# xDeepFM forward pass: the eighth broadcast pair moved from TensorE to DMA, with regrouped transfers, accumulator banks, gathers and dumps

## What is computed

```python
emb = tables[feat_idx, sparse]                     # (2048, 26, 32)
x0 = xk = emb
for w, bb in ((conv1_w, conv1_b), (conv2_w, conv2_b)):        # 128 rows each
    hp = einsum('bhd,bmd->bhmd', xk, x0).reshape(-1, h * 26, 32)
    xn = sigmoid(einsum('oi,bid->bod', w, hp) + bb[None, :, None])
    xk, keep = xn[:, :64], xn[:, 64:]              # keep is summed over the 32 and weighted
deep: tanh(x @ W1 + b1) -> tanh(@ W2 + b2) -> tanh(@ W3 + b3) -> @ deep_w   # 845 -> 1024 -> 512 -> 256
```

## Time and profile before

| | us |
|---|---|
| median of 3 runs (1628.97 to 1633.01) | 1631.12 |
| the profiled execution | 1624.22 |
| its span | 1622.4 |
| TensorE busy | 1543.6 (95%) |
| VectorE busy | 1104.7 (68%) |
| GpSimd busy | 709.2 (44%) |
| ScalarE busy | 643.5 (40%) |
| moved by DMA | 319.80 MB, 197 GB/s on average |

### The profile page before, as it was taken

One profiled execution on the slowest core, in us unless ns is written; L12 is line 12 of the kernel. 1 busy time (PEld: TensorE's weight loads), 2 busy tenths in 40 slices (PEclk: granted clock), 3 DMA queues, 4 the chain that ended last, 5 costly groups with the idle time before them and its releaser, 6 DMA issues.

```text
span 1622.4 us, 23599 instructions
## 1 busy us (share of the span) xinstructions
PE 1543.6 (95%) x6584; PEld 656.8 (40%) x6584; DVE 1104.7 (68%) x1017; ACT 643.5 (40%) x904; POOL 709.2 (44%) x600
## 2 busy tenths in 40 slices
PE   0598999999999999999999999999999999999999
PEld 0232333333333333333333333333333336787876
DVE  3276777777777877787777777787877783333332
ACT  2342434344434443434443434434343323344443
POOL 7356565556555556565555646464731110000000
PEclk9899999999999999999999999999999999999999
DMA  6688999999999999999998989898999884634531
GB/s 126 143 183 194 231 214 223 217 231 209 226 212 225 211 224 209 221 214 229 210 228 200 232 201 231 201 240 201 237 203 235 204 210 122 186 120 147 175 104 53
DMA packets 178599, 319.80 MB, mean 197 GB/s; under 512 B 31132, under 2 KB 106812, under 8 KB 178524
## 3 DMA queue, kind: packets, MB, share of 16 engines
q1 hardware_dynamic: 155423, 298.87, 75.0%
q10 hardware_dynamic: 9828, 13.43, 4.1%
q0 software_dynamic: 13312, 7.06, 3.8%
HBM read 297.93 MB, written 21.31 MB: 197 GB/s over the span
## 4 chain that ended last, share of the span: by engine, by line
PE 86%; issue 4%; DVE 3%; another core or an unknown queue 2%; POOL 2%; DMA 1%; SPq 1%; ACT 1%; ACTq 0%; DVEq 0%; POOLq 0%
PE y L751 42%; PE xn L745 19%; PE bc L880 16%; PE bc L731 5%; PE bc L738 3%; DVE hp L692 2%; POOL emb L542 2%; PE bc L723 1%; DVE xb L692 1%; SPq L465 1%; DMA x0t<-x_halves 1%; DMA x_lo<-dense_halves 0%; ACTq L370 0%; DMA emb<-table,idx_stage 0%
## 5 line engine op out<-in xcount | busy, mean ns | idle before, releaser
L692 DVE TENSOR_TENSOR hp<-bc,xk 128x1024 f32<-128x1024 f32 x384 | 453.9, 1219 | 271.3 <-PE bc L731 136.0
L542 POOL DMA_INDIRECT emb<-table,idx_stage x416 | 515.9, 1240 | 145.5 <-issue 126.3
L692 DVE TENSOR_TENSOR xb<-xb,xk 128x1024 f32<-128x1024 f32 x448 | 546.5, 1264 | 27.9 <-ACT xk L927 23.9
L751 PE MATMUL y<-xb,w2s 128*64 128x512 f32 x1792 | 436.0, 601 | 0.0
L745 PE MATMUL xn<-sq,w1s 128*128 128x512 f32 x768 | 369.7, 618 | 4.4 <-issue 4.4
L751 PE MATMUL y<-hp,w2s 128*64 128x512 f32 x1536 | 366.0, 597 | 0.0
L553 POOL TENSOR_TENSOR r<-r 128x512 f32<-128x512 f32 x96 | 123.5, 1287 | 351.0 <-ACT r L932 181.3
L926 ACT ACTIVATE xk<-xn,bias 64x512 f32<-64x512 f32 x128 | 87.4, 683 | 438.5 <-PE xn L745 248.8
L922 ACT ACTIVATE sq<-bc 128x1024 f32<-128x1024 f32 x192 | 182.9, 1026 | 197.5 <-PE bc L738 145.8
L751 PEld LDWEIGHTS y<-xb,w2s 128*64 128x64 f32 x1792 | 116.0, 136 | 248.8 <-issue 201.5
L745 PEld LDWEIGHTS xn<-sq,w1s 128*128 128x128 f32 x768 | 137.5, 192 | 162.6 <-issue 154.8
(11 more groups left out here) (57 smaller groups left out, 843.3 us busy)
## 6 DMA issues: line engine op xcount, KB each, us to landing
xb<-x_rows SPq DMA_DIRECT2D x896, 256.0 KB
w_raw<-W SPq DMA_DIRECT2D x32, 448.0 KB
x0t<-x_halves ACTq DMA_DIRECT2D x252, 52.0 KB
x_halves<-deep_halves SPq DMA_DIRECT2D x30, 384.0 KB
w_raw<-W SPq DMA_DIRECT2D x16, 512.0 KB
emb<-table,idx_stage POOLq DMA_INDIRECT x416
x_hi<-x_halves SPq DMA_DIRECT2D x24, 256.0 KB
x_lo<-x_halves SPq DMA_DIRECT2D x24, 256.0 KB
```

The lines of the kernel that those rows point to most:

```text
L542: nc.gpsimd.indirect_dma_start(out=emb[:, m, :], out_offset=None, in_=table, in_offset=bass.IndirectOffsetOnAxis(ap=idx_stage[:, m:m + 1], ...
L692: nc.vector.tensor_tensor(product(n)[:, :], x[:, :], xk[sl % 2][:, :], ALU.mult).then_inc(multiplied, 1)
L751: last = nc.tensor.matmul(y2[H * c:H * c + H, :], w2s[:, ORDER[n], :], src[:, c * CHUNK:(c + 1) * CHUNK], start=(n == 0), stop=(n == PAIRS ...
```

## The change

- `BY_PE` is now 3, 4, 5, 9, 10 and eight pairs go by DMA, in five groups `COPIED` = (0), (1, 2), (6, 7), (8), (11, 12). `ORDER`, which says which fields a pair number means, is permuted to suit.
- A group is three transfers: one field of each pair into partitions 32 to 95, the other into 0 to 31 and 96 to 127 (`PAIR_ROWS`). SyncE waits once a group, for its last pair, and VectorE waits for a group at its first pair.
- `STEP_WORK` puts both `contract_k` one behind the other, then fills 9, 10, then contracts 0 to 7 in one go; fills are (3, 4, 5) and (9, 10). All three parts of the transposed embedding go into one slot, in one fill.
- `xn` and `y2` become two banks `acc[0]`, `acc[1]` that change places each step: `contract_k(0)` writes the bank that this step's pairs are contracted into afterwards, `contract_k(1)` the other, once the last step's second layer has been read from it. The last step has an order of its own (`FINAL_WORK`), without the squares.
- `deep_step` is step 1 in tile 0 too; `dump_halves` and `dump` stand one behind the other at the end of step 1, after the broadcasts of that step.
- GpSimd's gathers: seven in a row ahead of the step-3 sum instead of three before it and four behind; in tile 0 all 26 for tile 1 are issued in step 0, the last 13 one by one after VectorE's products.
- The first loads of the deep part (`load_x(0)`) are spread over the four steps of the last tile.

```diff
-PAIR_ROWS = ((0, slice(0, H)), (1, slice(H, P)))
+PAIR_ROWS = ((1, slice(QUARTER, 3 * QUARTER)), (0, slice(0, QUARTER)), (0, slice(3 * QUARTER, P)))
-ORDER = [0, 1, 2, 3, 8, 4, 5, 9, 6, 7, 10, 11, 12]
-BY_PE = (3, 4, 6, 7, 9, 10)
+ORDER = [0, 1, 2, 3, 8, 4, 5, 6, 9, 10, 7, 11, 12]
+BY_PE = (3, 4, 5, 9, 10)
+COPIED = ((0,), (1, 2), (6, 7), (8,), (11, 12))
 STEP_WORK = (
     ("fill", (("K", 0), ("K", 1), ("K", 2))),
     ("of_last", (8, 9, 10)),
-    ("fill", (("D", 0), ("D", 1), ("D", 2))),
+    ("fill", (("D", 0),)),
     ("of_last", (11, 12)),
-    ("fill", (3, 4)),
+    ("fill", (3, 4, 5)),
     ("first", 0),
-    ("of_this", (0, 1, 2)),
-    ("fill", (6, 7)),
     ("first", 1),
     ("fill", (9, 10)),
-    ("of_this", (3, 4, 5, 6, 7)),
+    ("of_this", (0, 1, 2, 3, 4, 5, 6, 7)),
 )
-        xn = pb("xn", [P, CHUNK])
-        y2 = pb("y2", [P, CHUNK])
+        acc = [pb(f"acc{i}", [P, CHUNK]) for i in range(2)]
+        terms = acc[(STEPS - 2) % 2]
+        def first_acc(sl, c):
+            return acc[(sl + c) % 2]
             def spread_by_dma(t, sl, i):
+                ns = COPIED[i]
+                at = BY_DMA.index(ns[0])
+                fields = x0_rows[bass.ds(t, 1), :, :].rearrange("t (m e) b -> t m e b", e=ROW)
                 for f, parts in PAIR_ROWS:
-                    first = (2 * ORDER[BY_DMA[i]] + f) * ROW + sl * STEP_D
-                    row = x0_rows[bass.ds(t, 1), first:first + STEP_D, :].rearrange("t d b -> t (d b)")
-                    sp.dma_start(xb[i][parts, :], row.to_broadcast([parts.stop - parts.start, COLS])).then_inc(spread[i], 16)
+                    first, last = (2 * ORDER[n] + f for n in (ns[0], ns[-1]))
+                    rows = fields[:, first:last + 1:max(last - first, 1), sl * STEP_D:(sl + 1) * STEP_D, :]
+                    rows = rows.rearrange("t m d b -> t m (d b)").to_broadcast([parts.stop - parts.start, len(ns), COLS])
+                    dst = xb_all[parts, at * COLS:(at + len(ns)) * COLS].rearrange("p (m c) -> p m c", c=COLS)
+                    sp.dma_start(dst, rows).then_inc(spread[i], 16)
-                        if i == 2 and sl == 2 and not is_first and ahead > 0:
-                            dump_halves(t + 1)
-                    if sl == 2 and is_first:
+                    if sl == DEEP_STEP and ahead > 0:
                         dump_halves(t + 1)
-                    if sl == deep_step(ahead) and ahead > 0:
                         dump(t + 1)
-                    if sl == STEPS - 1 and ahead == 0:
-                        sp.wait_ge(dense_dumped, 64)
-                        load_x(0, 0, 1)
+                    if ahead == 0:
+                        if sl == 0:
+                            sp.wait_ge(dense_dumped, 64)
+                        load_x(0, sl, STEPS)
                         elif kind == "of_this":
-                            if what[0] == 0 and not start:
-                                pe.wait_ge(y2_read, s)
+                            if what[0] == 0:
+                                pe.wait_ge(xn_read, s * 2 + (2 if final else 3))
                         elif kind == "first" and not final:
                             if what == 0:
                                 pe.wait_ge(squared, squared_by(s, K1 - 1))
-                            pe.wait_ge(xn_read, s * 2 + (2 + what))
-                            contract_k(what)
+                            if what == 0:
+                                pe.wait_ge(xn_read, s * 2 + 2)
+                            elif not start:
+                                pe.wait_ge(y2_read, s)
+                            contract_k(what, first_acc(sl, what))
```

More of the change, by code:

```diff
@@ L52 @@
 PER_GROUP = 16
-ORDER = [0, 1, 2, 3, 8, 4, 5, 9, 6, 7, 10, 11, 12]
-BY_PE = (3, 4, 6, 7, 9, 10)
+ORDER = [0, 1, 2, 3, 8, 4, 5, 6, 9, 10, 7, 11, 12]
+BY_PE = (3, 4, 5, 9, 10)
 assert sorted(ORDER) == list(range(PAIRS))
-BY_DMA = tuple(n for n in range(PAIRS) if n not in BY_PE)
+COPIED = ((0,), (1, 2), (6, 7), (8,), (11, 12))
+BY_DMA = tuple(n for ns in COPIED for n in ns)
+assert sorted(BY_PE + BY_DMA) == list(range(PAIRS))
 STEP_WORK = (
@@ L81 @@
 HALF_DUMPS = 3
-def deep_step(ahead):
-    return 2 if ahead == 3 else 1
+DEEP_STEP = 1
 def step_fills(sl, ahead):
@@ L112, in group_of @@
     return int(2 * ORDER[n] >= PER_GROUP)
-assert all(group_of(BY_PE[i]) != group_of(BY_PE[i + 1]) for i in range(0, len(BY_PE), 2))
+assert all(group_of(n) != group_of(n + 1) for n in BY_PE if n + 1 in BY_PE)
 def fill_at(sl, use, ahead):
@@ L277, in build @@
         dumped = sem("dumped")
-        spread = [sem(f"spread{i}") for i in range(len(BY_DMA))]
+        spread = [sem(f"spread{i}") for i in range(len(COPIED))]
         filled = sem("filled")
@@ L575, in tile @@
                     gather(range(PAIRS), gathered)
+                    for n in range(PAIRS):
+                        pool.wait_ge(multiplied, n + 1)
+                        hold()
+                        gather((PAIRS + n,), gathered)
                 else:
                     if ahead > 0:
-                        gather(range(AHEAD[2], AHEAD[2] + 3), gathered)
+                        gather(range(AHEAD[2], M), gathered)
                     add_up(t - 1, STEPS - 1, r2, r2_step, y2_read, 1, sum2)
-                    if ahead > 0:
-                        gather(range(AHEAD[2] + 3, M), gathered)
@@ L781, in fill @@
                         pe.wait_ge(gathered, t * GATHERED + GATHERED)
-                    turn_deep(slot, DEEP_PARTS[use[1]])
+                    turn_deep(slot, [k for part in TURNS[use[1]] for k in DEEP_PARTS[part]])
             pe.wait_ge(ident_loaded, IDENT_LOADED)
@@ L794, in _ @@
             pe.wait_ge(squared, K1)
-            contract_k(0)
-            pe.wait_ge(xn_read, 1)
-            contract_k(1)
+            for c in range(2):
+                contract_k(c, first_acc(-1, c))
             pe.wait_ge(w2_loaded, W2_LOADED)
@@ L819, in tile @@
                     there = step_fills(sl, ahead)
-                    for kind, what in STEP_WORK:
+                    for kind, what in FINAL_WORK if final else STEP_WORK:
                         if kind == "fill":
@@ L970, in tile @@
                                             act.wait_ge(halves_dumped, t * (16 * HALF_DUMPS))
[L971 removed]
+                                    for part in TURNS[use[1]]:
+                                        turned_deep(slot_of(sl, use, ahead), part, DEEP_PARTS[TURNS[use[1]][0]][0])
                         elif kind == "of_last" and what[-1] == PAIRS - 1 and not start:
@@ L978, in tile @@
                         elif kind == "first" and ("K", 0) in there:
-                            late = is_first and sl == 2
-                            if what == int(late) and (sl < 2 or ahead > 0):
+                            if what == 0 and (sl < 2 or ahead > 0):
                                 if sl == 2:
```

110 lines of the change are left out of this document (54 added, 56 removed).

## The result

The changed kernel takes 1671.18 us (median of 4 runs, 1649.42 to 1676.45) against 1632.07 us for the kernel before, measured beside it (1628.97 to 1633.51). The ratio is 1.0208, with a 95% interval of 1.0125 to 1.0291; it is one of fast runs, without the 1676.45 us, which counts as slow, and with a fifth run of 1670.41 us (the quotient of the two medians would be 1.0240). The forecast was 1587 us, range 1575 to 1625. Both were missed, on the other side of no change. The profiled execution of the changed kernel took 1649.42 us, the lowest of its four.

The account below looks back on a forecast made before the run. The prediction took TensorE's program order as the bound, with DMA second, 5% behind. Its terms -31 (steps), +3 (stalls), -12 (start) and -3.7 (end) sum to -44 us: profiled 1580, median 1587 us, range 1575 to 1625.

Parts of the forecast that it names:

- 59 steady steps: Steady part, 59 steps: minus 31 us from a shorter TensorE step (16 to 34), plus 3 us of stalls.
- start: Prologue and tile 0: waits for a bank and for x0t go, minus 12 us (5 to 13).
- end: Last tile and deep part: waits for x loads and fills 9, 10 go, minus 3.7 us (1 to 4.5).
- TensorE's step: One steady step: one fill fewer and merged runs save 0.52 us (0.25 to 0.55), giving 18.85 instead of 19.37.
- The lone fill at 0.235: In fill (3, 4, 5), the lone pair costs 0.235 us, taken from the K fills, so the fill takes 0.67.
- the rival of the lone fill: The lone fill costs 0.43 and the bank change 0.1, so a step saves 0.25: 1602 us, chance 0.10.
- DMA, the deciding cost: Eight broadcasts a step want 254 GB/s; the engines give 270 (231 to 308), busy for 94% of a tile.
- The rival's own point of decision: DMA saturated: transfers across the halves no faster than in one, decisive from 254 GB/s downward; 1697 us, chance 0.12.
- Bursts late: Rate suffices (247 to 262 GB/s), but pairs 1 and 2 land late after the stores: 1617 us, chance 0.18.
- SyncE and the stores: Stores at the end of step 1 hold SyncE some 4 us: 0 to 1.5 us a tile, taken as 0.2.
- The 8.0 us for pairs 1 and 2: New broadcasts are needed 8.0 us after their contraction and arrive after 8 to 9; VectorE has about 2.5 us.
- ScalarE and the slot: Fill 5 waits for all copies: nothing, at worst 0.5 x 14 = 7 us; bank reads: 0 to 0.3 a step.

Follow-up runs that it names:

- the kernel with the same bytes in cheap transfers: The changed kernel with each group loaded by one transfer into all 128 partitions instead of three, second field of each pair left out: 1590.94 us, ratio 0.9767.
- the seven-pair kernel: The changed kernel with pair 6 back on TensorE, fills (3, 4) and (5, 6), seven pairs copied, stores in one block: 1704.24 us, ratio 1.0512.

## Why the prediction was wrong

The difference of the two profiled executions, 1649.42 - 1624.22 = +25.2 us, against the forecast's -44:

| term | forecast | measured | how |
|---|---|---|---|
| 59 steady steps | -28 | +25.1 | 1189.3 instead of 1164.3 |
| start | -12 | -5.2 | -1.8 until 69.64, then 69.3 instead of 72.7 |
| end | -3.7 | +5.3 | 42.5 to the deep part instead of 38.3, and +1.1 in it |

- **TensorE's step** was right: 18.81 without a stall. The lone fill at 0.235 holds, and with it the rival of the lone fill falls. 59 x 18.81 + 14.2 for transposes = 1124; the rest of 1189.3, 65 us, are stalls and what follows from them, where the prediction had 10. TensorE is idle for 48 of them (busy 1132.03 of 1180 us from 140 to 1320). About 11 more are the granted clock, at 0.50 behind some of the stops (an estimate from windows of 2 us): the run of three pairs that takes 2.79 us elsewhere takes 4.42 here. The stop of 2.20 us at 1011.17 left the clock full. The prediction had no term for this in the steady part; some 6 us aren't assigned. (Its bounds of 16 to 34 for 59 steps don't follow from 0.25 and 0.55 a step, which give 15 to 32; nothing hangs on it.)

```profile
1032.88 0.50 PE L745 MATMUL bc<-x0t,sel 32*128 32x512 f32 x4 [2.20 <-DVE hp L706]
1033.31 4.42 PE L765 MATMUL acc<-xb,w2s 128*64 128x512 f32 x12
```

- **"DMA, the deciding cost" is the step that failed.** Mis-sized is the rate: I took 270 GB/s, and it is 242. The one-half rate of 231 came from dividing (220 / 0.95); the full engines delivered 222 to 225 (two halves, eight pairs). With 223 and 311 the harmonic mean is 260. The changed kernel got 242 all the same; the 311 is itself divided out, from a share of 0.82, and no run shows that kind of transfer with full engines, so what takes the last 18 GB/s stays open. I took a value above the mean of the rows (264) for a resource that was wanted to 94%. The rival's own point of decision, "from 254 GB/s downward", was right, and 242 lies behind it; its price of 1697 belonged to 231. With 242, its formula gives 80.2 instead of 78.5 a tile, 15 x 1.7 = +26 us, and the steady part measured +25.1. That is no test of its own, since bytes over a measured rate must give the time; what tests it is the share of 1.00, and the kernel with the same bytes in cheap transfers at 0.9767. *Bursts late*, the other rival, asked for a rate between 247 and 262 and so didn't come true as put, but what it named, pairs 1 and 2 landing late, is what stops TensorE here too: VectorE's wait for them is 3.18 us where under 2.5 was to be seen.
- **"SyncE and the stores"**: the mechanism and the 4 us were right, the price of 0.2 us a tile was not. In the seven-pair kernel parting the stores is worth 57 us, some 4 us a tile, beyond the bound of 1.5. In the changed kernel it isn't visible (1.0183 against 1.0208); the engines stay full there, and ScalarE's late reads (22.8 us) take back part of what it may give.
- **The 8.0 us for pairs 1 and 2** was named as a limit, with arrivals at 8 to 9 us, and then priced at 3 us of stalls, stores included. It costs even with engines that aren't full: with seven pairs and a share of 0.86 the merged order still loses 1.8%, the old order with the same bytes wins 0.4% (what else differs between the two stands above). How much of the 65 us is rate and how much is this limit isn't parted. That cutting pair 0, ahead of 1 and 2, brought 1604 fits either.
- **ScalarE and the slot.** Fill (3, 4, 5) after the transposes waits 0.33 us for ScalarE's copies (forecast nothing, at worst 0.5): 4.6 us in 14 tiles. A wait of 0.45 for the read of the bank (bound 0.3) stands at 487.88; there are two of them, 1.1 us together. Both are small in this kernel; with the stores parted the second grows to 22.8 us.
- **Start.** Until the `contract_k` of 69.64 it won 1.8 (forecast 1.1). Then the last gather cost 4.20 instead of 2, and the slow clock lay on more work. That `contract_k` took 8.16 where 5.42 is usual (+2.7, forecast +2.2), and behind the wait for the gather the granted clock was 0.50 again, the lower of the two levels (1.2 GHz): transposes 1.73 instead of 0.98, two pairs 3.68 instead of 1.89. Two waits for products, 0.86 and 1.00 us, are the rest.

```profile
69.64 8.16 PE L759 MATMUL acc<-sq,w1s 128*128 128x512 f32 x12
...
93.07 1.73 PE L737 MATMUL bc<-idf,emb 128*128 128x128 f32 x7 [4.20 <-DMA emb<-table,idx_stage]
94.73 3.68 PE L765 MATMUL acc<-xb,w2s 128*64 128x512 f32 x8
```

Windows of the same stretches (the columns as above):

```profile
69.60:77.80 8.20, 8.20 (x18) 3.36 (x16) 6.61 (x6) 2.05 (x3) 6.23 (x5) 0.66 0.35 60
93.00:99.00 6.00, 5.93 (x21) 2.60 (x21) 0.00 (x0) 2.50 (x7) 0.00 (x0) 0.50 0.26 68
```

- **End.** The 2.80 us wait of the earlier trace rows is gone and 0.86 for `w_lo` came, as forecast (0.9). But the last tile has the broadcasts' waits too, with x loads beside them, and a slow clock behind the longest (two pairs in 3.67 us instead of 1.89):

```profile
1336.35 0.51 PE L745 MATMUL bc<-x0t,sel 32*128 32x512 f32 x4 [2.68 <-DVE hp L706]
...
1355.08 3.67 PE L765 MATMUL acc<-xb,w2s 128*64 128x512 f32 x8 [4.20 <-DVE xb L706]
...
1376.75 0.47 PE L895 MATMUL bc<-x_hi,w_hi 128*128 128x512 f32 x1 [0.86 <-DVE w_lo L677]
```

## What to carry to other kernels

Before work is moved from the busiest engine to DMA, ask what the queues must then deliver in the shorter step, and take for the rate a saturated one: a share of 0.95 divided out gave 231 GB/s where the full engines gave 222 to 225. An order that merges an engine's runs also moves the release of buffers; from the last release to the first need there must be room for the transfer and for all that is queued ahead of it, stores included. If a part of a change removes pressure without adding any (here the places, 0.85 of the engines instead of 0.95), run it alone: it won 0.4% where the whole lost 2.1%. And price a stop of the busiest engine with what it does to the clock: behind 3.65 us of idle the next contraction took 5.49 us instead of 2.84.

## What the runs showed of the hardware

- A 4 KB row of a transfer into partitions 32 to 95 took the engines a median of 159 ns, as one into all 128 did; in 0 to 63 it took 281 ns, and in 32 partitions at either end 266. The shares for the same bytes were 0.60, 0.76 and 0.74.
- Engines full of broadcasts delivered 222 to 225 GB/s in two halves and 236 to 245 GB/s with half of the bytes in 32 to 95 and half at the ends.
- Many partitions reading one and the same row of HBM cost nothing that reading distinct rows didn't (1649.42 to 1676.45 us against 1674.1 and 1705.02).
- Behind some stops of TensorE (3.65 us in the seven-pair kernel, one of 2.20 us in the changed one, but not another of 2.20 us) the granted clock stood at 0.50 for some us; in the seven-pair kernel with its stores in one block that cost about half as much again as the stops themselves.
- Waits of ScalarE of up to 11.0 us, once in many of the tiles, stand in all three traces from one chip; their releaser isn't in the profile, though TensorE's matmul records before them look as usual. The kernel before has them too (43.6 us in 8 times); in the 11 traces from three other chips there is none. Their cause wasn't found.
